# GpSimd's sends of tokens moved in an attention and expert kernel, and the routing spread over more steps

## What is computed

```python
xn = _layernorm(x, axis=-1)
x = x + _L0_attn_ref(xn, key, value, in_proj_weight, out_proj_weight) \
      + _L0_ffn_ref(xn, sg, su, sd, rg, ru, rd, wr, rb)

# _L0_ffn_ref
shared_out = _expert(x, sg, su, sd)        # silu(h @ g.T) * (h @ u.T) @ d.T, inner width 352
probs = jax.nn.softmax(x @ wr.T + rb, axis=-1)
scores, idx = jax.lax.top_k(probs, 2)
scores = scores / scores.sum(axis=-1, keepdims=True)
out = shared_out                            # + for each e: weight of e * _expert(x, rg[e], ru[e], rd[e])
```

## Time and profile before

| | |
|---|---|
| median of 3 runs | 471.19 us (468.56 to 472.63) |
| the profiled execution, its own time | 470.81 us |
| its span, first to last instruction | 469.0 us |
| busy: TensorE, VectorE, ScalarE, GpSimd | 436.3, 368.5, 311.4, 294.2 us |
| attention loop, step 0 to the last select | about 44 to 267 us of the span |
| experts | from 267 us on |

### The profile page before, as it was taken

One profiled execution on the slowest core, in us unless ns is written; L12 is line 12 of the kernel. 1 busy time (PEld: TensorE's weight loads), 2 busy tenths in 40 slices (PEclk: granted clock), 3 DMA queues, 4 the chain that ended last, 5 costly groups with the idle time before them and its releaser, 6 DMA issues.

```text
span 469.0 us, 12498 instructions
## 1 busy us (share of the span) xinstructions
PE 436.3 (93%) x3987; PEld 326.2 (70%) x3987; DVE 368.5 (79%) x810; ACT 311.4 (66%) x697; POOL 294.2 (63%) x415
## 2 busy tenths in 40 slices
PE   8978988988999999999888999999999999999995
PEld 4756656655666656666656678888888878888884
DVE  6985999999877887787777177777777888876887
ACT  2636766867677776777777766666767756666652
POOL 1425888888888888888888800447457576575200
PEclk9999899999999999999999999999999999999998
DMA  9786699999875665655539226867968867832762
GB/s 245 226 252 212 185 390 297 306 352 335 284 233 160 170 181 171 172 151 161 160 107 354 60 63 188 263 205 282 330 198 286 293 220 263 270 103 83 230 189 67
DMA packets 60415, 102.00 MB, mean 217 GB/s; under 512 B 11045, under 2 KB 29226, under 8 KB 59328
## 3 DMA queue, kind: packets, MB, share of 16 engines
q1 hardware_dynamic: 55872, 92.74, 62.2%
q0 software_dynamic: 4480, 8.47, 5.4%
HBM read 62.49 MB, written 39.46 MB: 217 GB/s over the span
## 4 chain that ended last, share of the span: by engine, by line
PE 54%; DVE 16%; issue 5%; POOL 5%; ACT 4%; DVEq 0%; POOLq 0%; ACTq 0%
PE ps L823 12%; PE ps L825 11%; PE ps L824 11%; DVE sb_blockmax L1314 7%; PE ps L891 4%; PE ps L952 4%; PE ps L899 3%; PE ps L1117 2%; POOL xs L589 2%; POOL sb_work L613 2%; ACT sb_work L691 2%; PE ps L1106 2%; PE ps L972 1%; PE ps L955 1%; DVE sb_on L1298 1%
## 5 line engine op out<-in xcount | busy, mean ns | idle before, releaser
L1314 DVE TENSOR_REDUCE sb_blockmax<-ps 128x6 f32<-128x768 f32 x128 | 121.7, 956 | 32.0 <-PE ps L899 25.8
L691 ACT ACTIVATE sb_work<-ps 128x768 f32<-128x768 f32 x128 | 104.1, 813 | 53.1 <-PE ps L887 51.8
L634 POOL DMA_INDIRECT ys<-sb_v_all,sb_xn_all x76 | 79.4, 1044 | 75.3 <-DVE sb_v_all L1435 57.0
L613 POOL TENSOR_SCALAR_AFFINE_SELECT sb_work<-sb_work 128x512 f32<-128x512 f32 x128 | 82.8, 649 | 24.2 <-ACT sb_work L691 21.9
L824 PE MATMUL ps<-sb_ring,sb_wb 128*128 128x512 f32 (+1 forms) x231 | 82.8, 358 | 0.0
L589 POOL DMA_INDIRECT xs<-sb_xn_all,sb_posu x64 | 62.9, 983 | 10.7 <-issue 10.7
L1414 DVE TENSOR_TENSOR sb_v_all<-ps,sb_v_all 128x512 f32<-128x512 f32 (+1 forms) x93 | 57.5, 618 | 14.2 <-ACT sb_v_all L771 9.7
L891 PE MATMUL ps<-sb_ring 32*128 32x256 f32 x256 | 49.4, 376 | 11.6 <-ACT sb_work L691 7.2
L771 ACT ACTIVATE sb_v_all<-ps 128x512 f32<-128x512 f32 (+1 forms) x93 | 49.8, 536 | 4.6 <-PE ps L825 3.9
L823 PE MATMUL ps<-sb_ring,sb_wb 128*128 128x512 f32 (+1 forms) x138 | 50.9, 369 | 0.0
L899 PE MATMUL ps<-sb_mask_b,sb_ident_b 128*128 128x256 bf16 x256 | 50.6, 279 | 0.0
(11 more groups left out here) (166 smaller groups left out, 1073.6 us busy)
## 6 DMA issues: line engine op xcount, KB each, us to landing
sb_wb<-wd SPq DMA_DIRECT2D x75, 384.0 KB, 4.0
sb_ring<-qk SPq DMA_DIRECT2D x64, 256.0 KB, 3.6
wd<-sb_wb SPq DMA_DIRECT2D x8, 1152.0 KB, 5.9
xs<-sb_o_all SPq DMA_DIRECT2D x19, 260.0 KB, 3.6
qk<-sb_ring SPq DMA_DIRECT2D x32, 128.0 KB
sb_work<-ys SPq DMA_DIRECT2D x16, 256.0 KB, 3.0
sb_xn_all<-xs SPq DMA_DIRECT2D x15, 260.0 KB, 3.5
sb_o_all<-w SPq DMA_DIRECT2D x8, 384.0 KB, 3.9
```

The lines of the kernel that those rows point to most:

```text
L613: pool.affine_select(out=o, in_=o, compare_op=ALU.is_ge, fill=0.0, base=0, pattern=[[0, 4], [1, 128]], channel_multiplier=-1)\
L634: pool.indirect_dma_start(out=ys_d, out_offset=bass.IndirectOffsetOnAxis(ap=row, axis=0), in_=yst[i % NYS][:, EMB * j:EMB * j + EMB], in_o ...
L691: act.activation(part.rearrange("p (k h q) -> p h k q", h=2, q=128), ps[:, 4:6, 0:HEAD].rearrange("p h (k q) -> p h k q", q=128), ACT.Exp, ...
L1314: dve.tensor_reduce(blockmax[:, a:b + 1, 0:3], ps[:, a:b + 1, 0:HEAD].rearrange("p h (k c) -> p h k c", c=128), AX.X, ALU.max).then_inc(s[ ...
```

## The change

The list of steps for the routing's pieces is longer: pieces 8 to 16 move from steps 10, 11, 13, 14, 15, 17, 18, 19, 21 to 11, 13, 14, 15, 17, 19, 21, 23, 25; the others stay. GpSimd's sends begin in step 26 instead of 23, and the loop up to step 62 has 56 of them instead of 64. The last eight (choice 1, tiles 24 to 31) are issued after the loop, four behind `attention_low(0)` and four behind `attention_low(1)`. `N_TURN`, worked out from `sent`, becomes steps 40 and 51 instead of 36 and 46. What SyncE waits for is the same.

Sends a step before, from step 23 on: 1, 2, 1, 2, 2, repeated. After, from step 26 on: 1, 2, 1, 2 and so on, with the twos in odd steps, and two in each of steps 61 and 62.

```diff
-        N_ROUTE = (0, 1, 2, 3, 5, 6, 7, 9, 10, 11, 13, 14, 15, 17, 18, 19, 21, 29, 33)
-        N_SEND = 23
+        N_ROUTE = (0, 1, 2, 3, 5, 6, 7, 9, 11, 13, 14, 15, 17, 19, 21, 23, 25, 29, 33)
+        N_SEND = 26
...
-        SENDS = TOPK * TILES
+
+        SENDS, LATE = TOPK * TILES, 8
 
         def sent(n):
-            return max(0, min(n, NQ - 2) - N_SEND + 1) * SENDS // (NQ - 1 - N_SEND)
+            return max(0, min(n, NQ - 2) - N_SEND + 1) * (SENDS - LATE) // (NQ - 1 - N_SEND)
...
             for c in range(EARLY):
                 attention_low(c)
+                sends(SENDS - LATE + LATE // EARLY * c, SENDS - LATE + LATE // EARLY * (c + 1))
```

## The result

The changed kernel takes 481.1 us (median of 4 runs, 477.64 to 481.91), the kernel before 470.46 (median of 4). The ratio is 1.0212, 95% interval 1.0172 to 1.0252: slower by 2.1%. The profiled execution took 481.91 us by its own time, with a span of 480.1.

A forecast was written before the change was run, and what follows sets the result against it. TensorE, busy 93%, was nearly full in the experts; the loop's chain lay on VectorE, then changed hands with TensorE and GpSimd. 470.81 - 1.6 (loop) + 8.9 (stop) + 1.7 (clock) = 479.8, forecast 480, range 476.5 to 483.5.

The forecast's parts named there:

- The bound: Routed experts, 276 to 400 us: TensorE works 122.81 of 124 us, so whatever stops it is paid in full.
- The eight sends: Behind the loop: last send ends at 279.3 instead of 265.30, tokens land at 284.2, TensorE stops +8.9 us (8.3 to 10.0).
- The second `attention_low` ... adds nothing.: Behind the loop: it moves behind four sends, but its reader `down(3)` follows the stopped transposes, so it adds nothing.
- The clock: Behind the stop: the clock falls to half for 3.41 us of dense matmuls, losing 1.7 us (0 to 3.4).
- rival 4: Behind the stop: the clock stays down twice as long, 481.5 us; inside the forecast's range, no separate chance.
- The loop: Attention loop of 64 steps: routing pieces moved and sends changed, in sum -1.6 us, ends -4.3 and +2.8.
- The sign named for it: Attention loop: the blocks of steps 8 and 16 would end at 13.5 to 14 us.
- Block 8: Steps 8 to 11, two routing pieces instead of three: gain 0 to 0.94 us, taken as 0.6, since VectorE alone holds it.
- a block can't fall below the one with no piece, 13.48, because TensorE and GpSimd then hold it: Attention loop: floor of 13.48 us for a block of four steps relieved of routing pieces.
- (1): Behind the loop: the tail hides the eight sends, leaving only the loop's gain, 469.2 us; chance 4%.
- (2): Stop comes without clock loss, and the loop gains all that VectorE frees, 474.8 us; chance 8%.
- (3): Attention loop: doubled sends in odd steps delay a select each time, making GpSimd the bound, 484.2 us; chance 10%.

The follow-up runs named there:

- the late sends alone: The changed kernel with the old `N_ROUTE` and `N_SEND = 23`, so only the last eight sends stay behind the loop; 479.25 us, 1.0184 to the kernel before.
- four late sends: The changed kernel with `LATE = 4`, two sends behind each `attention_low`; 472.57 us, 1.0053 to the kernel before.
- `LATE = 0`: The changed kernel with all 64 sends in steps 26 to 62, none behind the loop; 472.5 us, 1.0049 to the kernel before.
- the early writes: The kernel before with SyncE's 19 writes to the token list done by step 3 instead of step 19; 469.85 us, 0.9988.
- two sends between: The kernel before with two late sends between the two `attention_low`, nothing else changed; 473.22 us, 1.0048.
- the kernel with early writes: The changed kernel with list writes done by step 3 and two late sends between the two `attention_low`; 473.02 us, 1.0048 to the kernel before.
- the last run: The changed kernel with 30 unread matmuls of 512 columns in front of `tokens_in(2)`; 479.59 us, 1.0184 to the kernel before.

## Why the prediction was right, and where a step failed

The forecast was 480 (range 476.5 to 483.5), slower with a chance of 0.92; measured 481.1.

*The bound.* Right. TensorE was full behind the loop, and the stop was paid in full: nothing of the 9.0 us came back in the 195 us after it.

*The eight sends.* Right: +8.9 forecast, +9.0 measured, and +8.9 with the late sends alone. That it is so close is partly luck: inside it two terms were off and cancelled. The sends came every 1.27 us in place of 1.22 and the last one ended 12.9 us behind the last select, 0.6 later than forecast (12.3); SyncE's issue came 1.46 behind it in place of 2.1. The landing is 17.2 us behind the last select in both. Most of the 0.6 are two sends, of 1.29 and 1.12 us, that VectorE lengthened (a row of the section below). The prediction's sentence on the Trainium skill, page "DMA: Bandwidth & Descriptors", section "SWDGE vs HWDGE vs iDMA", had by its rule all sends at the upper end, 1.35; the other six took 0.96 to 0.99 with VectorE at work. So the trace agrees for two of the eight, 0.5 us in all.

*"The second `attention_low` ... adds nothing."* Wrong as a step, right in the sum. Its reader was indeed late anyway. But the subtraction moved from a time in which VectorE was idle to one in which it works, and held VectorE up by 1.7 us there (another row of that section); TensorE lost 1.20 us by it before L825. In the changed kernel that lies inside the stop. With fewer late sends it is the larger part of what is lost: 2.09 of 3.7 us with four, all of the idle time with two.

*The clock.* Right: 1.7 forecast; +1.3 measured in this profile, 2.72 / 2 = 1.36 by the work in the half-clock stretch, and 1.2 less with TensorE kept busy. With the late sends alone the fall held for twice as much work (rival 4's case). One reading was incomplete: the clock falls a second time in the trace before, at 466.59 us, but that is behind the last matmul and costs nothing here.

*The loop.* This step failed in its sign: -1.6 forecast, +0.8 measured in the profile, inside the ends given (-4.3 to +2.8). The sign named for it, blocks 8 and 16 at 13.5 to 14 us, did not come: 14.93 and 17.69. By stretches of the profile:

| part of the loop | forecast | measured |
|---|---|---|
| start to step 4 | 0 | -0.7 |
| steps 4 to 23 (blocks 8, 16, 20) | -1.3 | +2.5 |
| step 24 to the last select | -0.3 | -1.0 |

The first line is no effect of the change: the earlier trace rows shows a fall of the clock there which the profile after doesn't have. The second line has two parts. Block 8, down for -0.6 "since VectorE alone holds it", gained nothing in any profile of the new routing: "a block can't fall below the one with no piece, 13.48, because TensorE and GpSimd then hold it" named the wrong next one. In the changed kernel's profile the stores and loads of q and k hold the chain there; that they do so in every execution isn't shown. The DMA engines' share of these blocks stood in the earlier trace rows, 0.83 to 1.00 against 0.53 in the block taken as the floor, and I didn't read that column. Steps 12 to 23 gain 0.9 us where no fall of the clock lies in them, for -0.7 forecast, though not in block 16 alone. In this execution the fall in block 16 took 3.4 us away again; the sum allowed for a fall in the stop only. How close the profiled time comes to the forecast is therefore luck: the same program up to step 24, with four late sends, took 4.1 us less there, which would still have lain inside the range. By times nothing of the gain can be told from no change. In the third line one term was mis-sized: eight sends fewer over the same steps were valued at 0.6 us; they are worth 138.1 - 135.6 = 2.5 (`LATE` 0 against 8), 0.3 us a send, of which the later start takes 1.7 back (138.2 - 136.6).

*The rivals.* (1), the tail hides the sends, fell: of its limit, a last send 3.4 us behind the last select, even two sends behind both subtractions are short (4.9 us, transposes 0.9 us later). (2) fell by the 1.3 us of clock and by a loop that gained nothing in this profile. (3) fell by GpSimd's part in the loop: with the twos in odd steps the blocks of steps 44 and 48 last 13.60 and 13.59, against 13.48 and 13.85 in the earlier trace rows; no new bound.

The whole adds up another way too: the kernel with `LATE = 0` stands at 1.0049, the changed one at 1.0212, a difference of 7.7 us; the stop 9.0 and the clock 1.3, less 2.5 for the eight sends that left the loop, make 7.8. So the stop behind the loop is what makes the change slow.

*Open.* Why the loads of q and k are late by more in some executions of the same program than in others, and why the clock falls at some of these waits and not at others, isn't settled; moving the list's writes away from them didn't show it. No version tried beats the kernel before: two late sends behind both subtractions (1.0016) and the early writes (0.9988) can't be told from it. A third shared tile ahead of the routed ones, which would give the late sends more cover, wasn't tried.

## What to carry to other kernels

When work leaves a loop for the tail, measure the tail's slack from the trace first (here 5.1 us at the landing) and hold the moved work against it with its gaps: eight sends and what stands between them took 12.9 us, and the rest came out as a stop plus a clock at half behind it. When an engine that sets a block's length is relieved, read every column of that block, the DMA share too, before naming what comes next. And a small operation that is moved is to be checked against what runs beside it in the new place, not only against its own reader; here the trace of the kernel before held the price already (the section below).

## What the runs showed of the hardware

*GpSimd's subtraction holds VectorE.* VectorE's scaling L1300 (128x256, two inputs in SBUF) in the changed kernel, its timeline and its durations over the span (min, median, max in ns):

```profile
273.79 2.14 DVE L1300 TENSOR_TENSOR sb_on<-sb_xo,sb_rden 128x256 f32<-128x256 f32 x1
```

```profile
L1300 DVE TENSOR_TENSOR sb_on<-sb_xo,sb_rden x16: 424/553/2141, 65.7 to 273.8; 128x256 f32<-128x256 f32 x16
```

The 2.14 us are those beside GpSimd's second `attention_low`, 274.35 to 275.64; VectorE's instruction had begun before it and ended 0.29 us behind it. The 2.50 us above (0.69 without it) ended 0.57 behind. The trace of the kernel before has the same four times in its experts, so it could have been read ahead of the change. One of the four, GpSimd's and VectorE's lines:

```profile
375.65 1.32 POOL L623 TENSOR_TENSOR sb_xl_all<-sb_o_all,sb_xh_all 128x512 fp32r<-128x512 f32 x1
375.21 2.32 DVE L1421 TENSOR_TENSOR sb_ring<-sb_v_all,sb_qk_h 128x512 fp32r<-128x512 f32 x1
```

All four end 0.56 us behind GpSimd's subtraction. So the pattern is that a VectorE operation with two inputs in SBUF that meets GpSimd's subtraction ends its own usual time, less 0.13 us, behind the end of that one: 0.69 - 0.13 = 0.56, and 0.42 - 0.13 = 0.29 for L1300. That holds where VectorE's began up to 0.66 us earlier, and even for L1300, which by its usual 0.42 us would have been over 0.14 us before the subtraction's start; why its earlier start does not help, no run shows. The Trainium skill, page "GPSIMD Engine Reference", section "Key points", names this place: GpSimd shares its interfaces to SBUF with VectorE, and they contend where VectorE's instruction has two SBUF inputs. The traces agree, with these numbers.

*VectorE lengthens a send that begins inside such an operation.* The sends left VectorE's subtraction at 0.69 us, but not the other way round. The two long ones among the eight (273.03, 1.29 us; 279.62, 1.12 us) are those that begin inside VectorE's subtraction, VectorE's timeline:

```profile
272.80 0.69 DVE L1423 TENSOR_TENSOR sb_ring<-sb_v_all,sb_qk_l 128x512 fp32r<-128x512 f32 x1 [0.70 <-ACT sb_qk_l L780]
279.21 0.69 DVE L1423 TENSOR_TENSOR sb_ring<-sb_v_all,sb_qk_l 128x512 fp32r<-128x512 f32 x1 [0.70 <-ACT sb_qk_l L780]
```

It had 0.46 and 0.28 us to go, and the sends are 0.33 and 0.16 us above 0.96. In the trace of the kernel before, a scatter that begins at 319.15, with 0.56 us of that subtraction to go, takes 1.42 us instead of 0.98; one at 305.55, only 0.04 us behind the subtraction's start, takes 0.98.

*The clock falls inside the loop.* In the changed kernel a single wait of 2.2 us for a load was followed by 6.8 us at half clock, with TensorE busy all through: 3.4 us lost, 1.5 times the wait itself. The wait of 2.10 us with two sends between was followed by 3.4 us at half, the same wait of 2.12 us in the kernel with early writes by none, nor the two of 2.09 and 1.73 us with four late sends, 6 us apart. So a short wait costs itself alone or up to nearly three times itself (2.5 us of waiting and 10.2 at half in the last run, 9.4 of it with TensorE busy), and no run here shows which beforehand.
